# A fused decoder layer: the first turns of the attention pipeline in another order

## The chip, the core and the metric

The kernel runs on one core of a Trainium2 chip. A core has five engines, each with an instruction stream of its own: TensorE (PE in the rows; its weight loads are PEld), VectorE (DVE), ScalarE (ACT), GpSimd (POOL) and SyncE (SP), which here only issues DMAs. DMAs issued by SP, ACT and POOL are shown with a "q" behind the engine's name. The metric is the device time of one launch in microseconds, less is better. One execution was also recorded by the profiler; all views below read that one.

## The reference, cut to what matters

```
x = x + attn(layernorm(x))                 # x: 64 sequences, 128 tokens, width 128
x = x + xattn(layernorm(x), ctx_1024)      # context: 64 x 77 tokens, width 128, mask
x = x + ffn(layernorm(x))                  # 8 experts, the best 2 for each token
# attn and xattn: 16 heads of width 8
scores = einsum('bqhd,bkhd->bhqk', q, k)
attn   = softmax(scores)
out    = einsum('bhqk,bkhd->bqhd', attn, v) @ Wff.T + bff
```

## The kernel before

The 64 sequences are cut into 16 blocks of 4. Every block goes through a software pipeline of "turns": `steps` calls `body(t, t % 2)` on every engine for t = -3 to 17. A turn has two halves, x and y. In the x half of turn t TensorE does self-attention's shifted scores, and the products with the values, of block t beside the unshifted scores of block t + 1, of which VectorE takes the row maxima. In the y half it does the same for cross-attention: block t - 2 beside the maxima of block t - 1. `in_x(u)` and `in_y(u)` put the small work of other stages behind unit u (of 16) of a half: layer norm, transposes, projections, the gate. I write m(b), s(b), cm(b) and c(b) for the maxima and the attention proper of block b, in self-attention (m, s) and cross-attention (cm, c).

The way of one block into m(b), in self-attention:

1. SP loads `xin`; DVE `stats`, POOL `power`, ACT `normalise`; PE turns it over (`x1T`) and multiplies by w_q and w_k.
2. ACT, DVE, ACT and POOL (`first`, `remainder`, `second`, `third`) write each of q and k as three bf16 parts. SP `dump`s them to DRAM (`stk_q`, `stk_k`) and reads them back with `stack`, six DMAs each, in another layout into `qkbig` (`qs`, `ks`): rows 0 to 47 hold the parts of half of the heads, rows 64 to 111 those of the other half.
3. Three more rows of `ks` hold ones (`ones_under`). PE computes the scores of m(b) in 16 units of 4 matmuls of 128 columns (`scores`, two PSUM banks by turns), DVE reduces each unit (`maxima`).
4. POOL splits the negated maxima into three bf16 parts (`shares`), PE turns them over (`maxima_T`), ACT copies them to `parts_m`, and six DMAs (`fold`, or `first_folds` on ACT's queue for blocks 0 and 1) write them under `qs`. Only then can s(b) start: its scores (`shifted`) come out of PE with the maximum already taken off. ACT takes the exponentials (`attend`), PE multiplies by the values (`values`).

Cross-attention does the same with `cks` and `cqs` (`stack_cross`). The places of `cks` that hold an identity are written once by POOL (`places`). `gate` computes three small products that the router needs from the weights alone; before, it runs at the end of turn -1. Each engine runs its stream in order, so a wait holds back all that is behind it.

## Time and profile before

| | us |
|---|---|
| median of 3 runs | 1080.31 |
| the three runs | 1078.13, 1080.31, 1083.88 |
| time of the profiled execution | 1077.14 |
| its span (first to last instruction) | 1075.4 |
| PE busy in it | 904.4 (84%) |
| ACT busy | 796.5 (74%) |
| DVE busy | 781.5 (73%) |

The span is what the rows below cover; the profiled execution's own time is 1.7 us longer than its span and 3.2 us under the median. Busy PE time counts pipelined matmuls whose ends are modelled, so 84% doesn't say that PE is at its peak.

### The profile page before, as it was taken

How to read it: one execution, taken by the hardware profiler on the slowest of the kernel's cores; microseconds unless marked ns; L12 is line 12 of the kernel's file. 1: busy time of each engine (PE TensorE's matmuls, PEld its weight loads, DVE VectorE, ACT ScalarE, POOL GpSimd, SP SyncE). 2: the span in 40 equal slices, each digit the busy share in tenths (PEclk: the TensorE clock that was granted, in tenths of full speed). 3: DMA queues.
4: the chain of work that ended last, by engine and by line, in shares of the span. 5: the costliest groups of instructions: out<-in, count | busy, mean ns of one | idle time of the engine just before them, and what ended most of it. 6: DMA issues, size and time to landing. Idle time of an engine off the chain costs nothing.

```text
span 1075.4 us, 30453 instructions
## 1 busy us (share of the span) xinstructions
PE 904.4 (84%) x11109; PEld 661.0 (61%) x11109; DVE 781.5 (73%) x2190; ACT 796.5 (74%) x1652; POOL 648.1 (60%) x837
## 2 busy tenths in 40 slices
PE   2675778898998999889899888887878899999992
PEld 1343546666666666566576566665666677887771
DVE  3553756777886887877877768657638998998883
ACT  2153567778787878778788776777678899999981
POOL 2353333456676676766766654646556677777885
PEclk9996989999999999999999998999989999999996
DMA  4628877756777777677677664447223467779884
GB/s 99 133 56 158 149 122 151 164 111 146 167 128 150 156 137 158 136 139 162 127 152 152 128 129 100 91 128 153 65 63 102 150 212 237 248 209 255 233 225 127
DMA packets 108140, 158.82 MB, mean 148 GB/s; under 512 B 16829, under 2 KB 82000, under 8 KB 103384
## 3 DMA queue, kind: packets, MB, share of 16 engines
q1 hardware_dynamic: 93624, 130.25, 53.7%
q0 software_dynamic: 11184, 24.02, 9.2%
q10 hardware_dynamic: 3184, 2.60, 0.8%
q8 instruction: 89, 1.46, 0.6%
q14 instruction: 59, 0.48, 0.2%
HBM read 103.12 MB, written 53.78 MB: 146 GB/s over the span
## 4 chain that ended last, share of the span: by engine, by line
PE 50%; DVE 17%; DMA 9%; ACT 8%; issue 8%; POOL 5%; ACTq 1%; SPq 1%; POOLq 0%; DVEq 0%
PE pv L1799 8%; PE sc_m L1774 6%; PE wb L1751 6%; PE wb L1757 5%; PE wb L1746 4%; PE sc_a L1785 4%; DMA xg<-xs_d 3%; DVE negm_m L1185 3%; DVE on L1199 2%; DVE negm_cm L1185 2%; PE pv L2035 2%; PE pv L2028 2%; PE pv L2029 2%; DMA cbig<-parts_m 2%; ACT probs L934 2%
## 5 line engine op out<-in xcount | busy, mean ns | idle before, releaser
L934 ACT ACTIVATE probs<-sc_a 77x512 f32<-77x512 f32 (+1 forms) x512 | 302.1, 597 | 95.0 <-PE sc_a L1785 90.0
L689 POOL DMA_INDIRECT y_d<-yo,row x156 | 170.0, 1090 | 64.0 <-issue 41.6
L1185 DVE TENSOR_REDUCE negm_m<-sc_m 128x4 f32<-128x512 f32 x256 | 170.7, 683 | 42.7 <-PE sc_m L1774 39.9
L680 POOL DMA_INDIRECT xs_d<-xrow,slot_i x128 | 135.7, 1060 | 107.9 <-PE sc_a L1785 68.7
L1185 DVE TENSOR_REDUCE negm_cm<-sc_m 128x4 f32<-128x308 f32 x256 | 116.4, 471 | 77.9 <-PE sc_m L1774 76.2
L1799 PE MATMUL pv<-probs,big 128*32 128x128 f32 x4096 | 169.2, 284 | 3.9 <-issue 3.8
L1400 DVE TENSOR_TENSOR gl<-g,gh 128x512 fp32r<-128x512 f32 x156 | 107.0, 687 | 34.2 <-ACT g L1083 33.8
L1774 PE MATMUL sc_m<-qkbig 48*128 48x128 bf16 x1024 | 104.8, 233 | 26.9 <-DVE negm_m L1185 15.4
L1799 PEld LDWEIGHTS pv<-probs,big 128*32 128x32 f32 x4096 | 98.9, 111 | 38.8 <-ACT probs L934 12.6
L1774 PEld LDWEIGHTS sc_m<-qkbig 48*128 48x128 bf16 x1024 | 61.6, 100 | 94.9 <-DVE negm_m L1185 49.6
L1785 PE MATMUL sc_a<-qkbig 51*128 51x128 bf16 x1024 | 103.0, 227 | 8.6 <-ACT probs L934 7.2
L1785 PE MATMUL sc_a<-cbig 128*77 128x128 bf16 x1024 | 100.5, 222 | 1.9 <-ACT probs L934 1.5
L1774 PE MATMUL sc_m<-cbig 125*128 125x77 bf16 x1024 | 79.2, 200 | 14.7 <-DVE negm_cm L1185 8.1
L1774 PEld LDWEIGHTS sc_m<-cbig 125*128 125x128 bf16 x1024 | 59.6, 98 | 31.7 <-DVE negm_cm L1185 19.1
L1785 PEld LDWEIGHTS sc_a<-cbig 128*77 128x77 bf16 x1024 | 69.1, 118 | 4.7 <-ACT probs L934 3.4
L2035 PE MATMUL pv<-gl,vh 128*128 128x512 f32 x156 | 65.7, 421 | 5.9 <-DVE gl L1400 5.9
L1785 PEld LDWEIGHTS sc_a<-qkbig 51*128 51x128 bf16 x1024 | 60.1, 98 | 14.2 <-ACT probs L934 11.9
L668 POOL TENSOR_TENSOR parts_q<-rest_q,parts_q 128x512 bf16<-128x512 f32 x16 | 24.5, 1534 | 68.1 <-ACT parts_q L916 68.1
L1083 ACT ACTIVATE gh<-sc_m,bias 128x512 fp32r<-128x512 f32 x78 | 54.1, 693 | 13.8 <-issue 6.6
L2028 PE MATMUL pv<-gh,vh 128*128 128x512 f32 x156 | 62.0, 397 | 1.2 <-ACT gh L1083 1.0
L636 POOL TENSOR_SCALAR lnve<-lnmv 128x4 f32<-128x4 f32 x48 | 13.6, 284 | 79.9 <-DVE lnmv L1164 78.0
L2029 PE MATMUL pv<-gh,vl 128*128 128x512 f32 x156 | 61.3, 393 | 0.0
(240 smaller groups left out, 2302.6 us busy)
## 6 DMA issues: line engine op xcount, KB each, us to landing
wraw<-W_dram SPq DMA_DIRECT2D x39, 516.0 KB, 5.0
xg<-xs_d SPq DMA_DIRECT2D x39, 260.0 KB, 3.3
stk_q<-parts_q SPq DMA_DIRECT2D x16, 384.0 KB, 2.5
stk_k<-parts_k SPq DMA_DIRECT2D x16, 384.0 KB, 2.7
qkbig<-stk_q SPq DMA_DIRECT2D x32, 192.0 KB
qkbig<-stk_k SPq DMA_DIRECT2D x32, 192.0 KB
stk_cq<-parts_cq SPq DMA_DIRECT2D x16, 384.0 KB, 2.7
cbig<-stk_cq SPq DMA_DIRECT2D x32, 192.0 KB
```

The source lines that it names most:

```text
L680: nc.gpsimd.indirect_dma_start(out=xs_d, in_=xrow[b % 2][:, c // 2, c % 2, :], in_offset=None, out_offset=bass.IndirectOffsetOnAxis(ap=slo ...
L689: nc.gpsimd.indirect_dma_start(out=y12_d, in_=yo[i % NY][:, c, :], in_offset=None, bounds_check=2 * B * S - 1, oob_is_err=False, out_offse ...
L934: nc.scalar.activation(probs[e % 4][0:rows], sc_a[e % 2][0:rows], ACT.Exp, scale=scale)\
L1185: nc.vector.tensor_reduce(out=negm[n][:, s, HG * g + 4 * half:HG * g + 4 * half + 4], in_=sc_m[u % 2][:, 0:4 * cols].rearrange("p (j k) -> ...
L1400: nc.vector.tensor_tensor(out=gl[c], in0=g[c], in1=hi32(gh[c]), op=ALU.subtract).then_inc(gl_ok.sem, 1)
L1751: nc.tensor.matmul(wb[BANK[n]][:, 0:cols], lhsT, rhs, start=True, stop=True).then_inc(filled[n].sem, 1)
L1774: i = nc.tensor.matmul(sc_m[u % 2][:, j * cols:(j + 1) * cols], qst[rows, slot + j, s * S:(s + 1) * S], kst[rows, slot + j, s * cols:(s + ...
L1785: i = nc.tensor.matmul(sc_a[u % 2][0:cols, j * S:(j + 1) * S], kst[rows, slot + j, s * cols:(s + 1) * cols], qst[rows, slot + j, s * S:(s ...
L1799: i = nc.tensor.matmul(pv[s // 2][VW * c:VW * (c + 1), slot * S:(slot + 1) * S], va[:, HG * s + 4 * half + c, g, :], probs[u % 4][:, c * S ...
L2028: nc.tensor.matmul(o, vh[par][:, w], gh[c], start=(c == 0), stop=False)
L2029: nc.tensor.matmul(o, vl[par][:, w], gh[c], start=False, stop=False)
L2035: nc.tensor.matmul(y_banks[par][:], vh[par][:, c * 128:(c + 1) * 128], gl[c], start=False, stop=(c == FC - 1)).then_inc(w2_done.sem, 1)
```

## The change

Only the first turns are reordered:

- m(0) stays in the x half of turn -1, and m(1) follows in its y half, alone. m(0)'s `maxima_T` and fold come behind the third unit of m(1), and v of block 1 behind its thirteenth.
- Turn 0: x half s(0), alone on PE's side of the scores, with `maxima_T` of block 1 behind its second unit of shifted scores; y half s(1), beside the small work of block 0. Block 1's fold goes through SP's queue instead of ACT's.
- Turn 1: x half m(2), alone; then `maxima_T` of block 2, now ahead of cm(0); y half cm(0).
- From turn 2 on the order is the old one.
- `gate` moves from the end of turn -1 to the end of turn 0, the bias product with it.
- The ones rows of `ks` and `cks` are written first, in `constants`, and `xin` of block 1 is loaded between them instead of behind `dump("k", 0)`. The two copies of `places` move from turn -1 to turns -3 and -2.
- In turn 0 block 2's turning over, q and k come earlier (`FIRST_SELF`), and ck(0) behind k(2) on POOL; ck(0) is stacked earlier in SP's order. ACT waits for the last dump of q or k before it writes `parts_q` or `parts_k` again, in every turn.

```diff
--- before.py
+++ after.py
+SELF = dict(turn=8, q=10, k=13)
+FIRST_SELF = dict(turn=4, q=6, k=9)
+NORM1_OF = {0: 0}
...
+        def self_of(t):
+
+            return FIRST_SELF if t == 0 else SELF
+
+        def turned_maxima(t):
+
+            return {-1: 3, 1: 0}[t] if t in (-1, 1) else 7
...
+                    sp.wait_ge(ident_ok.sem, 7)
+                    for b in range(2):
+                        for g in range(NG):
+                            ones_under(ks[b], GP * g + KS, slice(0, HG))
+                        if b == 0:
+                            sp.wait_ge(ln_ok["1"].sem, ln_ok["1"].val(0))
+                            sp.dma_start(xin[:], x_v[1]).then_inc(x_in.sem, 16)
+                    for b in range(2):
+                        for g in range(NG):
+                            ones_under(cks[b], CS, slice(g * HG, (g + 1) * HG))
...
+                            if (n, t) != ("ck", 1):
+                                stack_cross(n, t - 1, dst[1 - par])
+                    if t == 0:
+                        fold(1, qs[1])
...
+                    if on_(t + 3) and t + 3 != 1:
...
+                    if t == 0:
+                        stack_cross("ck", 0, cks[0])
...
-                    if on_(t + 1):
+                    if t == 0:
+                        third("ck", t)
+                        mask_rows(t)
+                    if on_(t + 1) and t != 0:
...
+                    if t == -1:
+                        shares("m", 1)
...
-                steps(pool, body, {-2: numbers, -1: first_spare})
+                steps(pool, body, {-3: first_places, -2: numbers, -1: first_spare})
...
+                        if t == 0 and u == 3:
+                            evac(parts["m"][:], "m", 1, 0, rows=3 * H)
...
+                        if u == self_of(t)["q"] and on_(t + 2):
+                            if t + 2 >= 1:
+                                act.wait_ge(dumped["q"].sem, dumped["q"].val(t + 1))
...
-                    attend("s", t, 128, float(D) ** -0.5, in_x)
+                    attend("s", t if t != 1 else NONE, 128, float(D) ** -0.5, in_x)
...
-                    attend("c", t - 2, SC, float(DH) ** -0.5, in_y)
+                    if t == 0:
+                        attend("s", 1, 128, float(D) ** -0.5, in_y)
+                    else:
+                        attend("c", t - 2, SC, float(DH) ** -0.5, in_y)
...
-                    maxima("m", t + 1, S, in_x_too if t != -1 else None)
+                    maxima("m", t + 1 if t != 0 else NONE, S, in_x_too if t != -1 else None)
...
-                    maxima("cm", t - 1, SC, in_y)
+                    if t == -1:
+                        dve.wait_ge(split["m"].sem, split["m"].val(0, 2))
+                        maxima("m", 1, S, in_y)
+                    else:
+                        maxima("cm", t - 1, SC, in_y)
...
+                        if t == 0 and u == 2:
+                            maxima_T("m", 1)
...
-                    if on_(t):
-                        pe.wait_ge(drained["v"].sem, drained["v"].val(t))
-                        pe.wait_ge(stacked["m"].sem, stacked["m"].val(t))
-                        attn = ("s", t, qs[par], ks[par], vaug[par], S, ("c", t - 3))
-                    if on_(t + 1):
-                        for n in ("q", "k"):
-                            pe.wait_ge(stacked[n].sem, stacked[n].val(t + 1))
-                        if isinstance(t, int) and t + 1 < 2:
-                            pe.wait_ge(ones_in.sem, ones_in.val(t + 1))
-                        maxi = ("m", t + 1, qs[1 - par], ks[1 - par], S)
+                    if on_(t) and t != 1:
+                        attn = self_attention(t, ("c", t - 3) if t != 2 else ("s", 1))
+                    if on_(t + 1) and t != 0:
+                        maxi = self_maxima(t + 1)
...
+                    if t == -1:
+                        maxi = self_maxima(1)
+                    if t == 0:
+                        attn = self_attention(1, ("s", 0))
+                    if t == 1:
+                        maxima_T("m", 2)
...
-                steps(pe, body, {-1: gate})
+                steps(pe, body, {0: gate})
```

What stands in PE's stream behind m(0), before. `negm_m`'s splitting (`m_split`) is POOL's, `sc_m` are the scores for maxima, `sc_a` the shifted ones; L1824 is `maxima_T`, L1757 v of block 1, L1953 to L1958 the gate:

```order
L1774 MATMUL sc_m<-qkbig 128x128 [waits m_max_ok]
L1774 MATMUL sc_m<-qkbig 128x128 x3
L1824 MATMUL wb<-identb,third_m 48x128 [waits m_split,k_drained,m_max_ok]
L1824 MATMUL wb<-identb,third_m 48x128 x3
L1757 MATMUL wb<-w_v,xnT 128x128 [waits m_drained]
L1757 MATMUL wb<-w_v,xnT 128x128 x3
L1953 MATMUL wb<-ident,sim_u 128x8 [waits gate_set,v_drained]
L1955 MATMUL wb<-simT,wp_n 128x8 [waits gate_ev]
L1958 MATMUL wb<-cw_o,scrap 128x128 [waits gate_set,gate_ev]
L1774 MATMUL sc_m<-qkbig 128x128 [waits q_stacked,k_stacked,m_stacked,ones_in,v_drained,gate_set]
L1774 MATMUL sc_m<-qkbig 128x128 x7
L1785 MATMUL sc_a<-qkbig 128x128 x4
```

The same place of the changed kernel (L1822 are scores for maxima, L1886 is `maxima_T`):

```order
L1822 MATMUL sc_m<-qkbig 128x128 [waits m_max_ok]
L1822 MATMUL sc_m<-qkbig 128x128 x3
L1822 MATMUL sc_m<-qkbig 128x128 [waits k_stacked,ones_in,q_stacked,m_max_ok]
L1822 MATMUL sc_m<-qkbig 128x128 x7
L1822 MATMUL sc_m<-qkbig 128x128 [waits m_max_ok]
L1822 MATMUL sc_m<-qkbig 128x128 x3
L1886 MATMUL wb<-identb,third_m 48x128 [waits m_split,k_drained]
```

PE goes from m(0) to m(1) with a wait for block 1's q and k alone, and the maxima of block 0 are turned over three units later.

Between s(1) and m(2), the end of turn 0 in the changed kernel; L1847 are the products with the values, L2017 to L2022 the gate:

```order
L1799 MATMUL wb<-xnT,cw_q 128x512 [waits x2T_drained]
L1847 MATMUL pv<-probs,big 32x128 [waits exp_s_ok]
L1847 MATMUL pv<-probs,big 32x128 x3
L1847 MATMUL pv<-probs,big 32x128 [waits exp_s_ok]
L1847 MATMUL pv<-probs,big 32x128 x3
L2017 MATMUL wb<-ident,sim_u 128x8 [waits gate_set,v_drained]
L2019 MATMUL wb<-simT,wp_n 128x8 [waits gate_ev]
L2022 MATMUL wb<-cw_o,scrap 128x128 [waits gate_set,gate_ev]
L1822 MATMUL sc_m<-qkbig 128x128 [waits k_stacked,q_stacked,gate_set]
L1822 MATMUL sc_m<-qkbig 128x128 x7
```

The gate's three products now stand between the last product of turn 0 and the first scores of m(2), which wait for `gate_set`.

SP's stream from the last constant on, before:

```order
L423 DMA temp_b<-temp_dram 128x1
L428 DMA stk_q<-parts_q 128x3x512 [waits q_part3]
L428 DMA stk_k<-parts_k 128x3x512 [waits k_part3]
L491 DMA xin<-x_dram 128x4x128 [waits ln1_ok]
L447 DMA qkbig<-stk_q 24x4096 [waits q_dumped]
```

and in the changed kernel:

```order
L435 DMA temp_b<-temp_dram 128x1
L455 DMA qkbig<-ones 3x32x128 [waits ident_ok]
L455 DMA qkbig<-ones 3x32x128
L442 DMA xin<-x_dram 128x4x128 [waits ln1_ok]
L455 DMA qkbig<-ones 3x32x128 x2
L455 DMA cbig<-ones 3x32x77 x4
L450 DMA stk_q<-parts_q 128x3x512 [waits q_part3]
L450 DMA stk_k<-parts_k 128x3x512 [waits k_part3]
L466 DMA qkbig<-stk_q 24x4096 [waits q_dumped]
```

The load of `xin` for block 1 has moved ahead of both dumps, with eight small DMAs around it.

## Rows read from the trace of the kernel before

**Rows 1.** Busy time by stage; columns: stretch, length, busy us (instructions), clock, DMA, GB/s.

```profile
62.00:80.00 18.00, 17.11 (x274) 10.70 (x274) 12.04 (x19) 14.03 (x29) 5.16 (x6) 1.00 0.12 38
80.00:99.30 19.30, 7.25 (x36) 4.24 (x35) 5.39 (x22) 5.51 (x11) 7.77 (x15) 0.75 0.81 152
99.30:119.60 20.30, 18.19 (x278) 11.56 (x279) 14.15 (x23) 14.68 (x30) 6.23 (x6) 0.82 0.78 135
119.60:138.50 18.90, 11.49 (x104) 8.02 (x105) 11.89 (x38) 5.36 (x11) 7.16 (x15) 0.79 0.80 161
160.80:181.00 20.20, 18.28 (x304) 14.17 (x306) 11.88 (x38) 13.94 (x27) 6.11 (x12) 1.00 0.74 148
```

**Rows 2.** The chain that ended last, early part: start us, us, what.

```profile
88.91 10.32 DMA qkbig<-parts_m
...
125.94 10.95 DMA qkbig<-stk_k
...
138.48 0.60 PE sc_m L1774 x8
```

**Rows 3.** SP's DMA issues: start us, us, what.

```profile
20.36 0.38 SPq L428 DMA_DIRECT2D stk_k<-parts_k  x1
...
21.31 2.38 SPq L447 DMA_DIRECT2D qkbig<-stk_q  x6
...
27.39 1.29 SPq L447 DMA_DIRECT2D qkbig<-stk_k  x3
...
119.99 0.38 SPq L428 DMA_DIRECT2D stk_k<-parts_k  x1
...
121.67 2.37 SPq L447 DMA_DIRECT2D qkbig<-stk_q  x6
...
141.07 1.68 SPq L433 DMA_DIRECT2D cbig<-ones  x2
```

**Rows 4.** One stretch of 1 us, columns as in Rows 1.

```profile
37.00:38.00 1.00, 0.72 (x9) 0.38 (x8) 0.00 (x0) 0.60 (x1) 0.09 (x1) 1.00 0.00 0
```

**Rows 5.** PE in order of time: start us, us, what, [idle before, releaser].

```profile
37.60 0.62 PE L1774 MATMUL sc_m<-qkbig 48*128 48x128 bf16 x8 [0.28 <-issue]
...
51.18 0.59 PE L1824 MATMUL wb<-identb,third_m 128*48 128x128 bf16 x4 [2.25 <-POOL third_m L659]
52.45 2.08 PE L1757 MATMUL wb<-w_v,xnT 128*128 128x128 f32 x8 [0.68 <-ACT parts_m L888]
57.20 0.27 PE L1953 MATMUL wb<-ident,sim_u 8*128 8x8 f32 x1 [2.67 <-ACT big L1002]
...
61.96 0.30 PE L1774 MATMUL sc_m<-qkbig 48*128 48x128 bf16 x2 [2.56 <-issue]
```

**Rows 6.** PE at the start of turn 2's y half.

```profile
160.83 0.30 PE L1774 MATMUL sc_m<-cbig 125*128 125x77 bf16 x4 [1.26 <-DMA cbig<-parts_m]
```

**Rows 7.** DVE around the end of m(0) and the gate.

```profile
38.66 11.00 DVE L1185 TENSOR_REDUCE negm_m<-sc_m 128x4 f32<-128x512 f32 x16
49.58 0.86 DVE L1159 BATCH_NORM_STATS2 lnst<-xin 128x6 f32<-128x128 f32 x4
...
59.44 0.29 DVE L1672 TENSOR_TENSOR bo_b<-bo_b,wb 128x128 f32<-128x128 f32 x1 [3.89 <-PE wb L1958]
```

**Rows 8.** POOL's preset of the cks tiles.

```profile
53.01 8.53 POOL L794 COPY cbig<-identb 77x4928 bf16<-77x4928 bf16 x2
```

**Rows 9.** ACT's two roundings behind cross-attention's q product.

```profile
95.26 0.69 ACT L897 ACTIVATE parts_cq<-wb,bq_c 128x512 bf16<-128x512 f32 x1 [2.23 <-PE wb L1751]
96.83 0.63 ACT L916 ACTIVATE parts_cq<-rest_q 128x512 bf16<-128x512 f32 x1 [0.89 <-DVE rest_q L1175]
```

**Rows 10.** PE, matmuls of m(2) and s(1) side by side.

```profile
100.69 0.29 PE L1774 MATMUL sc_m<-qkbig 48*128 48x128 bf16 x1 [0.36 <-DVE negm_m L1185]
100.70 0.29 PE L1785 MATMUL sc_a<-qkbig 51*128 51x128 bf16 x1
```

**Rows 11.** The end of turn 1's y half, columns as in Rows 1.

```profile
130.50:136.00 5.50, 4.39 (x20) 2.16 (x18) 2.15 (x6) 2.55 (x7) 3.64 (x5) 0.50 0.80 141
```

More of the change, by code:

```diff
@@ L451, in stack_cross @@
                     sp.wait_ge(dumped[n].sem, dumped[n].val(b))
-                    if n == "ck" and b < 2:
-                        for g in range(NG):
-                            ones_under(n, dst, CS, slice(g * HG, (g + 1) * HG))
                     for place, skip in RUNS:
@@ L754, in body @@
                         third("q", t + 2)
-                    if on_(t):
+                    if on_(t) and t > 0:
                         third("ck", t)
@@ L947, in in_x @@
                     def in_x(u):
-                        if 2 <= u < 2 + NS and on_(t + 2):
-                            normalise("1", t + 2, xin, u - 2)
+                        if t == 0 and u == 3:
+                            evac(parts["m"][:], "m", 1, 0, rows=3 * H)
+                        at = NORM1_OF[t] if t in NORM1_OF else 2
+                        if at <= u < at + NS and on_(t + 2):
+                            normalise("1", t + 2, xin, u - at)
                         if u == 4 and on_(t - 3):
@@ L964, in in_x @@
                             fold(t - 2, cqs[par])
-                        if u == 8 and on_(t + 2):
+                        if u == self_of(t)["turn"] and on_(t + 2):
                             evac(xnT["1"][:], "x1T", t + 2, 0)
@@ L1109, in gate @@
                     nc.scalar.activation(wpx[:, D:D + E], wb[0][:, 0:E], ACT.Copy).then_inc(gate_ev.sem, 1)
-                steps(act, body, {-1: gate})
+                steps(act, body, {0: gate})
                 def last_block(i, c):
@@ L1292, in in_x @@
                             divide("c", t - 3, u)
-                        if u in MASKS and on_(t - 1):
+                        if u in MASKS and on_(t - 1) and t != 1:
                             masks(t - 1, cqs[1 - par], MASKS.index(u))
@@ L1299, in in_x @@
                             stats("3", t - 3, x3)
-                        if u == 11 and on_(t + 2):
+                        if u == self_of(t)["q"] + 1 and on_(t + 2):
                             wait_block(dve, part3["cq"], t - 1)
@@ L1305, in in_x @@
                             remainder("ck", t, bk_c)
-                        if u == 14 and on_(t + 2):
+                        if u == self_of(t)["k"] + 1 and on_(t + 2):
                             wait_block(dve, part3["k"], t + 1)
@@ L1310, in in_y @@
                     def in_y(u):
+                        if t == 0 and u in MASKS:
+                            masks(0, cqs[0], MASKS.index(u))
                         if u < NO and on_(t):
@@ L1672, in output_bias, with beside_context @@
                     nc.vector.tensor_tensor(out=bo_b[:], in0=bo_b[:], in1=wb[0][:, 0:D], op=ALU.add).then_inc(gate_set.sem, 1)
-                def beside_and_bias():
+                def beside_context():
                     ones_beside(cvaug, "cv", SC)
-                    output_bias()
-                steps(dve, body, {-3: beside_first, -2: gate, -1: beside_and_bias})
+                steps(dve, body, {-3: beside_first, -2: gate, -1: beside_context, 0: output_bias})
                 def late_base():
@@ L1818, in beside, with self_attention, self_maxima @@
                             between(u)
+                def self_attention(b, last):
+                    pe.wait_ge(drained["v"].sem, drained["v"].val(b))
+                    pe.wait_ge(stacked["m"].sem, stacked["m"].val(b))
+                    return "s", b, qs[b % 2], ks[b % 2], vaug[b % 2], S, last
+                def self_maxima(b):
+                    for n in ("q", "k"):
+                        pe.wait_ge(stacked[n].sem, stacked[n].val(b))
+                    if b < 2:
+                        pe.wait_ge(ones_in.sem, ones_in.val(3))
+                    return "m", b, qs[b % 2], ks[b % 2], S
                 def maxima_T(n, b):
@@ L1860, in in_x @@
                             maxima_T("cm", t - 2)
-                        if u == 8 and on_(t + 2):
+                        if t == 0 and u == 2:
+                            maxima_T("m", 1)
+                        if u == self_of(t)["turn"] and on_(t + 2):
                             pe.wait_ge(ln_ok["1"].sem, ln_ok["1"].val(t + 2))
@@ L1886, in in_y @@
                             project("s", t, w_ff)
-                        if u == 6 and on_(t + 1):
+                        if u == turned_maxima(t) - 1 and on_(t + 1) and t not in (0, 1):
                             maxima_T("m", t + 1)
```

58 lines of the change are left out of this document (29 added, 29 removed).

## The prediction

> **What bounds the kernel now.** I read the profile's page first, then windows by stage, the chain of waits, SP's DMA issues and PE's stream in order of time. The page gives PE 84% of the span, but that is an average over 20 turns, and the change touches only those that end by about 181 us. So the question is: when does turn 2 begin, before and after? Behind it the order of work is the old one, and what shifts its start shifts the end.
>
> [Rows 1] show stages of two kinds. In those in which two halves' work lies side by side (62 to 80, 99.3 to 119.6, 160.8 to 181) PE is busy for 17.11 to 18.28 of 18 to 20.3 us: PE-bound. In 80 to 99.3 PE works 7.25 of 19.30 us and DMA is at 0.81: that is the wait for block 1's fold, which the chain of waits shows as 10.32 us of DMA [rows 2]. In 119.6 to 138.5 DMA is at 0.80 again, and the chain goes through 10.95 us of block 3's q and k being stacked before turn 2's x half starts at 138.48 [rows 2]. So before turn 2 the kernel is bound by turns by PE and by the transfers that PE's next half needs.
>
> The first stage is a DMA stage too. SP begins to stack block 0's q at 21.31 [rows 3], the DMA engines go quiet at 37 [rows 4], and m(0) begins at 37.60 [rows 5]: 16.3 us from the first stack issue to PE. For block 3 the same took from 121.67 [rows 3] to at most 138.48, at which PE starts [rows 2]: at most 16.8, and by the end of the chain's DMA (125.94 + 10.95 = 136.89) 15.2. I use 15.2 to 16.3 as the price of stacking a block.
>
> **The change, step by step.** Times are those of PE from the start of the span.
>
> 1. *xin(1) and the ones rows first.* Before, xin(1) is issued between k(0)'s dump (20.36) and the first stack (21.31) [rows 3], and shares the 16 engines with the stacks of block 0. Now it goes some 11 us earlier, when they have little to do. Its 128 x 4 x 128 x 4 bytes are 0.26 MB; the twelve stacks move 96 rows of 4096 x 2 bytes for each of q and k, 1.57 MB. So xin is 14% of the 1.84 MB, 2.3 of 16.3 us; with one issue less ahead of the stacks I take 2.5: m(0) starts at 35.1. Bounds: 0 (the packets of the stacks themselves set the time) and 3. The ones DMAs are small; two cost SP 1.68 us of issue [rows 3], 0.84 each. All eight now lie ahead of the dumps, where SP otherwise waits.
>
> 2. *m(1) behind m(0).* m(0) took 37.60 to 49.66 (38.66 + 11.00, [rows 5, 7]), 12.1 us. With 12.1 it now ends at 47.2. Block 1's q and k come out about 6 us earlier than before, because their input does, and their first stack issue falls at about 36; plus 15.2 to 16.3 gives 51.2 to 52.3; I take 51.7 for m(1)'s start. So PE waits some 4.5 us there. m(1) costs the 12.1 less 0.7 for its first unit, whose results DVE need not wait for, plus v of block 1 (2.08 us of PE in [rows 5], of which I take 1.4; bounds 0.7 and 2.1) and block 2's layer norm statistics on DVE (0.86, [rows 7], up to 1.3 with what waits for it): about 14.0, so it ends at 65.7 to 66. Fold(0) needs m(0)'s maxima_T behind the third unit of m(1): it lands near 61, hidden behind m(1).
>
> 3. *x half of turn 0: s(0) alone.* It took 18.0 with m(1) beside it [rows 1]. What m(1) gave up is less than its count of instructions: in [rows 10] a score matmul of m and one of s start 0.01 us apart on different partitions and take 0.29 each, so they ran side by side and splitting them gives little back. New in this half is maxima_T of block 1, which waits for POOL's shares; after m(0) it waited 2.25 us from the last product and began 1.5 behind the last maximum (49.66 to 51.18, [rows 5, 7]), so I add 1.3 when two units of s(0) are ahead of it, less what the missing evictions give. I take 18.3; bounds 16.5 and 19.5. End: 84.3. Fold(1) is issued near 70 and takes at most the 10.32 of [rows 2]: landed by 84. This is the change's gain: the 19.30 us of 80 to 99.3 held 12 us without PE work.
>
> The Trainium skill, TensorEngine Tiling (Array Packing), Overview, says that the array can work as several independent tiles, up to twice as fast for contractions of 64 rows or fewer. By that rule taking m and s apart costs up to all of m's matmuls again, 64 of 0.29 us, where a reader who adds up busy time would expect the total to stay. The trace agrees for these two.
>
> 4. *y half of turn 0: s(1) beside in_y(0).* The nearest full half is 160.8 to 181, 20.20 us [rows 1], in which the scores of cm ran too: 16 units of 0.30 [rows 6] are 4.8. That gives 15.4; I take 15.7, bounds 15 and 17. End: 100.0.
>
> 5. *gate.* Before, it stood in a gap that was there anyway: its first product at 57.20 came 2.67 us after v for want of ACT, DVE's end of it is at 59.44 + 0.29 = 59.73, and s(0) waited for the fold until 61.96 [rows 5, 7]. Cover gone, its price is 59.73 − 57.20 = 2.5, and ahead of it on ACT stands now the rounding of cq (the two of [rows 9] are 1.57 us from start to start, PE idle 2.23 before the first), of which 1.3 shows. Together 3.8; bounds 2.5 and 4.7. Queued behind it on PE is m(2), which waits for gate_set. Block 2's stack has landed by 100 to 102, so the gate and not the DMA sets m(2): 103.8, that is 4.5 later than before (99.3).
>
> 6. *x half of turn 1: m(2) alone*, beside in_x: 12.1 of m(0) is its floor, and in_x adds transposes and the projections of block 3. I take 15; bounds 13.3 and 17. End 118.8. k(3)'s dump lay 0.4 us behind the end of this half (119.99 against 119.6, [rows 1, 3]). ACT's and DVE's chain to it doesn't shrink as much as PE's, so I take 1.7 behind: 120.5.
>
> 7. *maxima_T(2) ahead of cm(0).* It waits for POOL's third of k and then the shares: +3.3 (the 1.5 of m(0), and 1.8 of POOL work ahead of it; bounds 1.5 and 4.5), to 122.1. Then cm(0), which before took from 119.6 to about 136 [rows 1, 11]: 16.3, so PE would be ready at 138.4. The DMA way is later by a little: from dump to x(2) 138.48 − 119.99 = 18.5 [rows 2, 3], so 120.5 + 18.5 = 139.0. Fold(2), issued near 124 and 10 long, is hidden.
>
> 8. *The rest.* The two ones DMAs at 141.07 (1.68, [rows 3]) leave turn 2; its y half began after 1.26 us of waiting for cbig's DMA [rows 6], so −1.0, bounds 0 and −1.26. ACT's new wait for the dumps in every turn: it is there for a transfer that was issued a turn's part earlier, +0.3 in all, bounds 0 and 1.7. `places` (8.53, [rows 8], 4.27 each) goes to turns in which POOL only waits for input: nothing; if the cover were gone, 4.3 on block 1's third parts, which would eat most of the 4.5 us that m(1) already waits.
>
> Sum: +0.5 (139.0 against 138.5) − 1.0 + 0.3 = −0.2. The profiled execution's 1077.14 becomes 1076.9. It lies 3.2 under the median of the three runs, so the forecast for a median is 1080.31 − 0.2 = **1080.1 us**. In words: 12 us of PE's waiting at 80 to 99.3 are bought with a wait of 4.5 ahead of m(1), two gaps at the gate and maxima_T (7.1), and a turn whose start goes by DMA as before.
>
> **The rivals.** What a measurement of this kernel can tell from no change is about 0.5%, 5.4 us: faster is below 1074.9, slower above 1085.7.
>
> *Faster: block 1 lands early, and the lone halves are short.* If a landing goes by the last stack issue rather than by bytes, m(1) starts 2.2 us earlier (49.5); s(0) alone takes 16.5 instead of 18.3, and m(2) 13.3 instead of 15. That is −5.7, and it reaches turn 2 because k(3)'s dump comes with m(2)'s end: 1080.1 − 5.7 = 1074.4, and 1071.5 with the gate at its low end as well. For it: the lone halves lack half of PE's instructions (274 in 18 us, [rows 1]). Against: ACT's exponentials alone are 14 us of each s half [rows 1], and [rows 10]. It begins to count as faster when all three terms hold. Chance 0.22.
>
> *Slower: TensorE at half clock in m(2) and cm(0).* Granted clock is 0.75 and 0.79 in the stages in which PE waits, and 0.50 at 130.5 to 136 [rows 1, 11]: the lower of its two levels, 1.2 of 2.4 GHz, after PE had worked 7.25 of 19.30 us or 11.49 of 18.90. The change gives turn 1 two PE-light halves in a row with the gate's gap ahead of them. Then m(2) takes 17, not 15, the gate's gap 4.7, maxima_T 4.5, and x(2) starts on a low clock, +1 to +2: +5 to +6.5, some 1085.1 to 1086.6. It decides from about 5.6 us on. Chance 0.14.
>
> The Trainium skill, TensorE: Matmul & The Clock Gate, says that TensorE's clock is gated to 1.2 GHz when it is idle. By that rule this rival is what the gate gap and the two lone halves invite; the granted clock in the rows falls after idle stretches, which agrees.
>
> *It doesn't do what it says: turn 2 is fixed by block 3's stack.* If k(3)'s dump depends on xin(3) and the projections rather than on PE's order, x(2) starts within 1 us of 138.5 whatever came before: 1079 to 1081. Chance 0.10.
>
> **How the numbers follow.** The forecast as summed has 0.52, its own range 1077 to 1084 (step 1 at 0: +2.5; steps 3, 4 and 6 at either end partly cancel). With the last rival and 0.02 for the rest, within 0.5% has 0.64, faster 0.22, slower 0.14. The range from 1071.5 to 1086.5 leaves about 0.1 out at each end.
>
> **What the changed profile would show.** m(0) near 35.1 and m(1) near 51.7, with a wait for DMA between; s(0) at 66, s(1) at 84.3 with no DMA wait; a gap of 2.5 to 4.7 us with the gate in it, its releasers ACT and DVE, and m(2) at 103.8; maxima_T(2) waiting for POOL at 119 to 122; x(2) at 139.0 released by DMA, or PE. The prediction is wrong if m(1) starts before 49 or after 55, if a lone half takes as long as a double one (20 us), if m(2) is released by a stack, or if x(2) starts more than 5 us from 138.5. It is wrong in another way if x(2) starts there and the end moves all the same: then a wait was added in every turn.

## The result: about 1% slower

| | us |
|---|---|
| changed kernel, median of 4 runs | 1094.28 (1090.35, 1091.42, 1097.13, 1097.86) |
| kernel before, median of 4 runs beside it | 1082.10 (1078.13, 1080.31, 1083.88, 1089.56) |
| ratio | 1.0098, 95% interval 1.0051 to 1.0145 |
| profiled execution of the changed kernel | 1090.35, span 1088.6 |

The interval lies wholly above 1: 5.5 to 15.7 us more. Ratios here and below leave out runs more than 1.5% above their kernel's fastest. The kernel before had medians of 1084 us beside the first eight of the further runs, 1105 beside the next three and 1109 beside the last, so times are only compared with those taken beside them. The profiled executions are 13.2 us apart, and turn 2 starts 10.1 us later (138.48 to 148.56), so most of the difference is there when the order becomes the old one again. The rest, 3 us, is less than the runs of one kernel differ by.

I read the changed kernel as the prediction laid it out, PE in order of time. First its wait for block 1 (compare [rows 5]):

```profile
37.77 0.62 PE L1822 MATMUL sc_m<-qkbig 48*128 48x128 bf16 x8 [6.31 <-issue]
...
54.76 0.62 PE L1822 MATMUL sc_m<-qkbig 48*128 48x128 bf16 x8 [6.08 <-DMA qkbig<-stk_k]
...
67.38 0.39 PE L1822 MATMUL sc_m<-qkbig 48*128 48x128 bf16 x2 [0.77 <-DVE negm_m L1228]
67.49 0.37 PE L1833 MATMUL sc_a<-qkbig 51*128 51x128 bf16 x2
```

m(0) starts when it did before (37.60 then, 37.77 now), PE waits 6.08 us for block 1's k, and s(0) begins at 67.49 against 61.96. SP shows why m(1) can't be earlier:

```profile
20.64 2.33 SPq L466 DMA_DIRECT2D qkbig<-stk_q  x6
23.02 2.22 SPq L466 DMA_DIRECT2D qkbig<-stk_k  x6
31.26 0.39 SPq L450 DMA_DIRECT2D stk_q<-parts_q  x1
34.88 0.38 SPq L450 DMA_DIRECT2D stk_k<-parts_k  x1
35.31 0.48 SPq L510 DMA_DIRECT2D xin<-x_dram  x1
38.38 2.14 SPq L466 DMA_DIRECT2D qkbig<-stk_q  x6
```

Block 0's stack takes 20.64 to 37.77 and block 1's 38.38 to 54.76: one behind the other, 17.1 and 16.4 us. SP issues the second only when m(0)'s first unit is done (its wait on `max_f` stands in the code of both kernels).

The end of turn 0, with the gate in the open, and the end of turn 1:

```profile
103.01 1.10 PE L1799 MATMUL wb<-xnT,cw_q 128*128 128x512 f32 x2 [0.31 <-ACT xnT L921]
104.03 0.64 PE L1847 MATMUL pv<-probs,big 128*32 128x128 f32 x16
104.61 0.22 PE L2017 MATMUL wb<-ident,sim_u 8*128 8x8 f32 x1
106.46 0.39 PE L2019 MATMUL wb<-simT,wp_n 128*128 128x8 f32 x2 [1.63 <-ACT simT L1150]
107.11 0.79 PE L2022 MATMUL wb<-cw_o,scrap 128*128 128x128 f32 x2 [0.27 <-ACT wpx L1152]
108.29 0.61 PE L1822 MATMUL sc_m<-qkbig 48*128 48x128 bf16 x8 [0.38 <-DVE bo_b L1721]
...
125.28 0.62 PE L1822 MATMUL sc_m<-qkbig 48*128 48x128 bf16 x8
130.52 0.59 PE L1886 MATMUL wb<-identb,third_m 128*48 128x128 bf16 x4 [4.62 <-POOL third_m L679]
...
146.03 1.10 PE L1799 MATMUL wb<-xnT,cw_q 128*128 128x512 f32 x2 [0.64 <-ACT xnT L921]
148.56 0.41 PE L1822 MATMUL sc_m<-qkbig 48*128 48x128 bf16 x8 [1.43 <-issue]
```

From the last product of turn 0 to m(2) there are 3.7 us; from the last unit of m(2) to the turned-over maxima PE waits 4.62 us for POOL. By stage, cut at the starts of the halves (columns as in [rows 1], to which they answer):

```profile
54.76:67.38 12.62, 9.98 (x73) 6.57 (x73) 10.21 (x23) 1.68 (x3) 1.71 (x4) 1.00 0.03 8
67.38:86.90 19.52, 16.40 (x218) 9.79 (x219) 6.90 (x9) 14.32 (x29) 8.64 (x11) 1.00 0.24 78
86.90:104.60 17.70, 14.81 (x223) 9.92 (x222) 7.01 (x25) 12.75 (x26) 4.45 (x9) 1.00 0.76 155
104.60:108.30 3.70, 1.42 (x10) 0.94 (x7) 1.03 (x2) 2.85 (x9) 1.88 (x2) 0.84 0.05 12
108.30:126.00 17.70, 15.86 (x86) 8.49 (x86) 10.33 (x17) 4.10 (x9) 2.86 (x3) 0.50 0.56 106
126.00:130.50 4.50, 0.00 (x0) 0.01 (x1) 1.81 (x3) 0.39 (x2) 3.56 (x7) 0.50 0.35 122
```

Two rows carry the result. s(0) alone takes 19.52 us; with m(1) beside it the half took 18.00 [rows 1]. And m(2) alone, 86 matmuls where the shared half of before had 278, takes 17.70 us at a granted clock of 0.50. The halves that were thinned did not become short. For s(0)'s half ScalarE (14.32 us busy of 19.52) doesn't explain all: PE also waited 1.82 us for POOL at 70.23, ahead of block 1's turned-over maxima, and a group of 16 products with the values took 1.08 us at 71.31 and 74.50, and 0.64 from 77.35 on; before, the groups took 0.64 already from 69.19 on. No run takes these apart.

### The profile page after: what moved, and what is told of

The parts are those of the page before. It is cut to its first block, busy times and chain, and to the rows that moved or that the text cites. A ratio compares the mean times of both kernels' runs of the same rounds, so it can differ in the third digit from the quotient of the medians.

```text
span 1088.6 us, 30485 instructions
## 1 busy us (share of the span) xinstructions
PE 923.4 (85%) x11109; PEld 674.9 (62%) x11109; DVE 786.0 (72%) x2190; ACT 795.7 (73%) x1652; POOL 646.5 (59%) x837
## 4 chain that ended last, share of the span: by engine, by line
PE 52%; DVE 17%; issue 9%; ACT 8%; POOL 6%; DMA 5%; SPq 2%; ACTq 1%; POOLq 0%; DVEq 0%
PE pv L1847 8%; PE sc_m L1822 7%; PE wb L1799 6%; PE wb L1805 5%; PE sc_a L1833 4%; PE wb L1794 4%; DVE negm_m L1228 2%; DVE negm_cm L1228 2%; DVE on L1242 2%; DMA xg<-xs_d 2%; PE pv L2099 2%; PE pv L2093 2%; PE pv L2092 2%; ACT probs L967 2%; DVE lnst L1202 1%
## 5 line engine op out<-in xcount | busy, mean ns | idle before, releaser
L1847 PE MATMUL pv<-probs,big 128*32 128x128 f32 x4096 | 169.1, 285 | 2.2 <-issue 2.2
L1822 PE MATMUL sc_m<-qkbig 48*128 48x128 bf16 x1024 | 106.2, 239 | 35.3 <-DVE negm_m L1228 17.3
L1822 PEld LDWEIGHTS sc_m<-qkbig 48*128 48x128 bf16 x1024 | 62.1, 102 | 101.7 <-DVE negm_m L1228 51.8
L1847 PEld LDWEIGHTS pv<-probs,big 128*32 128x32 f32 x4096 | 99.1, 111 | 38.8 <-ACT probs L967 12.9
L1833 PE MATMUL sc_a<-qkbig 51*128 51x128 bf16 x1024 | 99.7, 227 | 8.6 <-ACT probs L967 8.3
L1822 PE MATMUL sc_m<-cbig 125*128 125x77 bf16 x1024 | 80.2, 203 | 10.6 <-DVE negm_cm L1228 7.8
L1822 PEld LDWEIGHTS sc_m<-cbig 125*128 125x128 bf16 x1024 | 60.9, 100 | 27.5 <-DVE negm_cm L1228 19.2
L1833 PEld LDWEIGHTS sc_a<-qkbig 51*128 51x128 bf16 x1024 | 58.2, 97 | 20.2 <-ACT probs L967 16.3
L659 POOL TENSOR_TENSOR lnrs<-lnve,mhalf 128x4 f32<-128x4 f32 x48 | 55.2, 1150 | 4.0
```

The source lines that it names most:

```text
L1822: i = nc.tensor.matmul(sc_m[u % 2][:, j * cols:(j + 1) * cols], qst[rows, slot + j, s * S:(s + 1) * S], kst[rows, slot + j, s * cols:(s + ...
L1833: i = nc.tensor.matmul(sc_a[u % 2][0:cols, j * S:(j + 1) * S], kst[rows, slot + j, s * cols:(s + 1) * cols], qst[rows, slot + j, s * S:(s ...
L1847: i = nc.tensor.matmul(pv[s // 2][VW * c:VW * (c + 1), slot * S:(slot + 1) * S], va[:, HG * s + 4 * half + c, g, :], probs[u % 4][:, c * S ...
```

## The experiments

Theory at the start: the loss is a sum of exposed work in turns -1 to 1 (m(1) alone, the gate, the clock), carried to the end. Rivals: the gate or the early maxima alone do it; ACT's new waits cost in every turn; turn 2 is pinned by transfers whatever precedes it. Nothing separates kernels here better than 0.3 to 0.5%, so I read each twice: the ratio to the kernel before, and the places in its profile. One profile is one execution; where the clock fell in it moves the later places by some us (last section).

**The gate between m(0) and m(1).** In each engine's stream the call moves to turn -1:

```diff
                     if t == -1:
+                        gate()
                         maxi = self_maxima(1)
...
-                steps(pe, body, {0: gate})
+                steps(pe, body)
```

> The changed kernel with the gate (and the bias product and its addition) between m(0) and m(1), where PE waits 6.1 us for block 1's k; all else as changed. Theory (the gate's 3.7 us between s(1) and m(2) lie on the path, and the clock's fall at 107 us comes with that pause): m(2) starts at 104.6 to 105 in place of 108.29, turn 2's x half 3.7 to 8 us before the changed kernel's 148.56, the time 4 to 8 us under the changed kernel's 1090 to 1098. Rival (turn 2 is fixed by the transfers of block 3, whatever stands ahead): m(2) earlier, but x(2) within 1 us of 148.56 and no change of time. Second rival (the gate's wait is not hidden in the new place either): m(1) later than 54.76 by 1 us or more.

Ratio to the kernel before 1.0139 (1.0061 to 1.0218).

```profile
48.78 0.27 PE L2021 MATMUL wb<-ident,sim_u 8*128 8x8 f32 x1 [0.79 <-DVE negm_m L1230]
49.32 0.60 PE L2023 MATMUL wb<-simT,wp_n 128*128 128x8 f32 x2 [0.27 <-ACT simT L1152]
50.18 0.79 PE L2026 MATMUL wb<-cw_o,scrap 128*128 128x128 f32 x2 [0.27 <-ACT wpx L1154]
55.14 0.62 PE L1825 MATMUL sc_m<-qkbig 48*128 48x128 bf16 x8 [4.17 <-DMA qkbig<-stk_k]
...
104.56 2.04 PE L1802 MATMUL wb<-xnT,cw_q 128*128 128x512 f32 x2 [0.24 <-ACT xnT L921]
106.53 1.08 PE L1850 MATMUL pv<-probs,big 128*32 128x128 f32 x16
107.55 0.62 PE L1825 MATMUL sc_m<-qkbig 48*128 48x128 bf16 x8
```

The gate disappears in the wait for DMA, and m(2) follows the values without a pause. But it starts at 107.55, only 0.7 earlier: in this execution the clock fell at the end of turn 0 already, and cq's product takes 2.04 in place of 1.10. So the clock does not need the gate's pause to fall, and that half of the theory is gone. The next two runs have the gate where the change put it, and there too it read 0.50 from about 103 us on, before the gate. The gate's price is seen against the next run, where the clock fell as early: m(2) at 111.45 there, 107.55 here, 3.9 us. In the time it can't be seen.

**Block 2's maxima turned over in cm(0) again.**

```diff
-            return {-1: 3, 1: 0}[t] if t in (-1, 1) else 7
+            return 3 if t == -1 else 7
...
-                    if t == 1:
-                        maxima_T("m", 2)
```

> The changed kernel with the turned-over maxima of block 2 back behind the seventh unit of cm(0) in place of ahead of cm(0). Theory (turn 2's start is fixed by the stacks of block 3 and the fold of block 2, which land at 147.2 and 148.6 and which SP issues only from 130.7 on): cm(0) starts 4.5 us earlier, at 126.0 to 126.5 in place of 131.05, but x(2) stays within 1.5 us of 148.56, and the time within 0.3% of the changed kernel's. Rival (the 4.62 us that PE waits for POOL's third_m are on the path): x(2) at 144 to 145 and the time 4 to 5 us less.

Ratio 1.0100 (1.0062 to 1.0137), the changed kernel's own. The scores of cm(0) come 1.40 us after those of m(2), not 4.6, and PE then waits at the end for what it gained:

```profile
128.14 0.39 PE L1822 MATMUL sc_m<-qkbig 48*128 48x128 bf16 x4 [0.44 <-DVE negm_m L1228]
129.94 0.44 PE L1822 MATMUL sc_m<-cbig 125*128 125x77 bf16 x4 [1.40 <-DVE negm_m L1228]
...
144.39 1.10 PE L1799 MATMUL wb<-xnT,cw_q 128*128 128x512 f32 x2 [0.63 <-ACT xnT L921]
150.67 0.62 PE L1822 MATMUL sc_m<-qkbig 48*128 48x128 bf16 x8 [5.18 <-issue]
```

5.18 us of waiting stand ahead of turn 2 where the changed kernel has 1.43. But m(2) itself began 3.2 us later in this execution (111.45), so turn 2 at 150.67 is outside the 1.5 us that the theory gave it. Counted from m(2) it comes 39.2 us behind, 40.3 in the changed kernel and 39.0 in the run with the gate moved, which has the pause too: the pause of 4.62 us cost nothing that can be seen.

**Unused matmuls in the pauses.** 26 behind the gate's first product and 40 ahead of `maxima_T`:

```diff
+                def keep_busy(n):
+                    for _ in range(n):
+                        nc.tensor.matmul(sc_a[0][:, 0:128], identb[:], identb[:], start=True, stop=True)
```

> The changed kernel with matmuls that compute nothing that is used: 26 of 128x128 in bf16 behind the gate's first product and 40 ahead of the turned-over maxima of block 2, both into a PSUM bank that is free then, so that PE does not pause there. Theory (m(2) takes 17.7 us because the granted clock is 0.50 in it, and the clock fell because PE paused at the gate): the clock record stays 1.00 in m(2), whose length falls to 13 to 14.5 us; x(2) 3 to 5 us earlier than 148.56. Rival (the clock falls for another reason, or m(2) is bound by DVE and ACT and not by PE's clock): m(2) still 17 to 18 us long, or the clock at 1.00 and the length unchanged; the time the same or up to 2 us more.

Ratio 1.0150 (1.0090 to 1.0210), an interval that overlaps the changed kernel's. m(2)'s half, cut at 112.2 and 130:

```profile
112.20:130.00 17.80, 15.19 (x80) 8.04 (x78) 11.16 (x18) 4.45 (x9) 2.39 (x3) 0.53 0.59 102
```

The clock is 0.53, and m(2) itself, 111.84 to 129.12, takes 17.3 us. In this execution the clock fell at about 103, ahead of the gate; behind the 26 unused matmuls it read 1.00 again from 110 to 112, and from 114 on 0.50: filling the pauses didn't keep the clock up. The rival holds as far as the pauses go. What the half would take at the full clock stays untried, but in the four profiles in which this half holds the same work, it is the shorter the higher its mean clock: 17.6 us at 0.50 (the changed kernel), 17.3 at 0.54 (here), 17.1 at 0.57 (maxima late), 16.3 at 0.60 (gate moved). That speaks for the clock having a part in its length; it isn't tested by itself.

**Ones rows and xin first, alone**, in the kernel before (with ACT's waits for the dumps):

```diff
+                    sp.wait_ge(ident_ok.sem, 7)
+                    for b in range(2):
+                        for g in range(NG):
+                            ones_under(ks[b], GP * g + KS, slice(0, HG))
+                        if b == 0:
+                            sp.wait_ge(ln_ok["1"].sem, ln_ok["1"].val(0))
+                            sp.dma_start(xin[:], x_v[1]).then_inc(x_in.sem, 16)
...
+                                act.wait_ge(dumped["q"].sem, dumped["q"].val(t + 1))
```

> The kernel before with one part of the change alone: the ones rows written first, xin of block 1 loaded between them, and ACT's wait for the dumps of q and k (in every turn), which that order needs. The order of the turns, the gate and the places are those of before. Theory (these parts cost nothing, the order of the first turns does): the time within 0.4% of before, x(2) at 137 to 139.5 against 138.48, m(0) at 37.2 to 38 against 37.60. Rival (ACT's new wait is paid in every turn and explains the distance that grows behind turn 2): the time 3 us or more above before, with ACT's idle time before the first part of q or k released by a dump, in each turn.

> The kernel before with the ones rows and xin of block 1 first, a second time, with more rounds: is it faster than before, or the same? Theory (turn 2 starts 2 us sooner): the time 1 to 3 us under before. Rival: no difference that can be measured.

Ratios 0.9965 (0.9915 to 1.0016) and 1.0014 (0.9980 to 1.0048): no difference that can be measured. So neither the early ones, nor xin, nor ACT's waits in every turn explain the loss. m(0) stays at its place, but s(0) comes 2.8 us earlier than before, and turn 2 at 136.09 and 136.76 against 138.48 (the first theory had it at 137 or later):

```profile
58.02 0.79 PE L1966 MATMUL wb<-cw_o,scrap 128*128 128x128 f32 x2 [0.27 <-ACT wpx L1117]
59.20 0.62 PE L1782 MATMUL sc_m<-qkbig 48*128 48x128 bf16 x8 [0.38 <-DVE bo_b L1680]
...
96.73 0.62 PE L1782 MATMUL sc_m<-qkbig 48*128 48x128 bf16 x8 [2.86 <-DMA qkbig<-parts_m]
```

**The wait that the change removes, removed alone.** In the kernel before, ACT writes block 1's rows at the start of turn 0, from block 0's maxima:

```diff
+                    if t == 0:
+                        act.wait_ge(stacked["m"].sem, stacked["m"].val(0))
+                        first_folds(0, qs[1])
                     attend("s", t, 128, float(D) ** -0.5, in_x)
```

> The kernel before without the wait that the change removes: the rows that block 1's shifted scores need are written early, at the start of turn 0, from block 0's maxima (so block 1's attention is computed with the wrong maximum; its output is not the reference's). Theory (behind the fold another wait of the same length stands: block 2's stack, which lands at 98.6 us against the fold's 99.2, and ahead of both in_y(0)'s own chain, whose last product on PE ends at 95.2): turn 1's x half starts at 98 to 99.3, at most 1.5 us earlier than 99.32. Rival (the step of the prediction that counted 12 us of the 19.30 as a gain): it starts at 92 or earlier.

One run: 1076.56, beside a median of 1083.76 (1075.15 to 1108.20) for the kernel before. (A softmax doesn't depend on which number is taken off a row, so what is computed differs only in rounding.) The end of the stage, before:

```profile
93.18 2.05 PE L1751 MATMUL wb<-xnT,cw_q 128*128 128x512 f32 x2 [0.78 <-ACT xnT L888]
99.32 0.62 PE L1774 MATMUL sc_m<-qkbig 48*128 48x128 bf16 x8 [4.10 <-DMA qkbig<-parts_m]
```

and in this run:

```profile
94.00 2.04 PE L1756 MATMUL wb<-xnT,cw_q 128*128 128x512 f32 x2 [0.78 <-ACT xnT L888]
100.14 0.62 PE L1779 MATMUL sc_m<-qkbig 48*128 48x128 bf16 x8 [4.09 <-DMA qkbig<-stk_k]
```

This is the row of the study. The fold's wait is gone, and PE waits 4.09 us for block 2's k instead; turn 1 starts at 100.14, not earlier than the 99.32 of before. The edit has a cost of its own: ScalarE now issues the six DMAs at 61.19 (3.91 us), inside s(0)'s half, and that half's last copy (`oT`) comes at 81.30 instead of 79.69. From that copy to turn 1 it is 18.84 us against 19.63, so in its own stage the wait was worth 0.8 us, and not 12.

**And block 2's q and k earlier too** (as `FIRST_SELF` does in the change):

```diff
+            return {0: dict(turn=4, q=6, k=9)}.get(t, dict(turn=8, q=10, k=13))
```

> As the run without block 1's fold (its output is not the reference's for the same reason), and turn 0's turning over, q and k of block 2 four units earlier, as in the change, with ck(0) behind k(2) on POOL. Theory (with the fold and the stack both out of the way, in_y(0)'s chain from DVE's divisions to PE's cq product is what is left of the 19.3 us): turn 1's x half starts at 95 to 97, right behind the cq product, 2 to 4 us before 99.32 and no more. Rival (turn 1 waits for the transfers only): 91 to 94, before the cq product is due.

```profile
93.51 2.05 PE L1763 MATMUL wb<-xnT,cw_q 128*128 128x512 f32 x2 [0.78 <-ACT xnT L894]
95.81 0.62 PE L1786 MATMUL sc_m<-qkbig 48*128 48x128 bf16 x8 [0.26 <-DMA qkbig<-stk_k]
```

With both waits out of the way turn 1 starts 0.3 us behind the last product of `in_y(0)`, at 95.81: in_y(0)'s own chain of small work fills what is left. Turn 1 is 3.5 us earlier than before, and from the copy of `oT` (80.80) to turn 1 it is 15.0 us, 4.6 less: that is what both waits together were worth. And it wasn't kept: turn 2 came at 140.19, later than before, and the one run took 1081.01.

**Block 3's q and k earlier in turn 1**, in the changed kernel and in the kernel before with xin first:

```diff
-            return FIRST_SELF if t == 0 else SELF
+            return FIRST_SELF if t == 0 else dict(turn=5, q=7, k=10) if t == 1 else SELF
```

> The changed kernel with block 3's turning over, q and k three units earlier in turn 1 (5, 7, 10 in place of 8, 10, 13) and ck(1) behind k(3) on POOL. Theory (from the start of m(2) to turn 2 it takes 38.7 to 41 us in every kernel so far, with s(1) in that half or not, because k(3) comes out of in_x at unit 13 and its dump, stack and the fold behind it then take 19): k(3)'s dump comes 2.5 to 4 us sooner after m(2)'s start, and turn 2's x half 36 to 37.5 us behind m(2)'s start; the time 2 to 4 us under the changed kernel's. Rival (turn 1 is bound by PE at half clock and the pauses): 39 to 41 us from m(2) to turn 2 as before.

> The kernel before with the ones rows and xin of block 1 first (as in the run that had these alone) and, in turn 1 alone, q and k of block 3 three units earlier (5, 7, 10 in place of 8, 10, 13) with ck(1) behind k(3) on POOL; the order of the halves is that of before. Theory (turn 2's start hangs on block 3's stack): turn 2's x half 36 to 37.5 us behind turn 1's instead of 39, at 133 to 135.5 us, and the time 3 to 6 us under the kernel before. Rival (in_y(1)'s chain or cm(0) bounds turn 1's y half): 38.5 to 39.5 us behind and a time within 0.3% of before.

Ratios to the kernel before 1.0091 (1.0055 to 1.0126) and 0.9972 (0.9934 to 1.0010): no change against their bases. Neither theory held; the rivals came closer (turn 2 is 40.3 and 39.8 us behind turn 1). In the first, k(3)'s dump is issued 17.8 us behind m(2)'s start in place of 20.9, but turn 2 starts at 147.95, 40 us behind m(2), since PE runs through its own work without a wait before it. In the second the shared half took longer:

```profile
96.00:118.50 22.50, 19.95 (x258) 11.95 (x259) 14.02 (x23) 14.20 (x29) 6.53 (x6) 0.67 0.63 126
```

So my theory that turn 1's 39 us hang on k(3) fell: with k(3) earlier, PE at a low clock (0.67 in this row) had no idle time ahead of turn 2 to give back.

**m(1) ahead of s(0), but s(1) back beside m(2)** (gate ahead of m(1), maxima as before):

```diff
-                    if on_(t) and t != 1:
-                        attn = self_attention(t, ("c", t - 3) if t != 2 else ("s", 1))
+                    if on_(t):
+                        attn = self_attention(t, ("c", t - 3))
...
-                    if t == 0:
-                        attn = self_attention(1, ("s", 0))
```

> One half of the reordering alone: m(1) stays ahead of s(0), alone behind m(0), as in the change; but s(1) goes back beside m(2) in turn 1's x half, as before, so that the y half of turn 0 holds only in_y(0). The gate stands ahead of m(1) and block 2's maxima are turned over behind the seventh unit of cm(0), so that neither weighs here. Theory (taking m(1) out of s(0)'s half costs about 5 us at s(0) and is not given back, since s(0) alone is no shorter than with m(1); moving s(1) costs the rest): s(0) at 67 to 68.5, turn 1's x half at 102 to 105, when block 2's stack has landed, against 99.7 before and 108.3 to 112 in the kernels with the whole reordering; turn 2's x half 39 to 41 us behind that, at 142 to 145; the time 3 to 6 us above before. Rival (the loss is all in m(1)'s new place): turn 2's x half at 147 or later, the time 10 us above before.

Ratio 1.0075 (1.0040 to 1.0110).

```profile
66.44 0.62 PE L1822 MATMUL sc_m<-qkbig 48*128 48x128 bf16 x8
67.83 0.39 PE L1822 MATMUL sc_m<-qkbig 48*128 48x128 bf16 x2 [0.77 <-DVE negm_m L1227]
...
101.36 2.05 PE L1799 MATMUL wb<-xnT,cw_q 128*128 128x512 f32 x2 [0.78 <-ACT xnT L921]
103.34 0.62 PE L1822 MATMUL sc_m<-qkbig 48*128 48x128 bf16 x8
...
142.34 0.62 PE L1822 MATMUL sc_m<-qkbig 48*128 48x128 bf16 x8 [2.21 <-issue]
```

The profile's places are the theory's: s(0) at 67.8, turn 1 at 103.3, turn 2 at 142.3. By the time, this half of the reordering costs 0.75%, 4.4 to 12.2 us at the 1105 that the kernel before took beside it: both the theory's upper end and the rival's 10 are inside. What is safe is that m(1)'s new place makes the kernel slower without s(1)'s; its 0.75% is three quarters of the changed kernel's 0.98%, though the intervals overlap, and the two were timed beside different runs of the kernel before.

**ck(0) stacked at the end of turn 0**, on top of xin first, twice:

```diff
+                    if t == 0:
+                        stack_cross("ck", 0, cks[0])
```

> The kernel before with the ones rows and xin of block 1 first, and block 0's ck stacked in SP's stream at the end of turn 0, as in the change, in place of the start of turn 1 (DMA engines have less to do then, and cm(0) waits for cq's stack, which goes behind it). Theory (turn 2 hangs on block 3's stack, not on cm(0)): cm(0) up to 2.5 us earlier than in the kernel with xin first alone, turn 2's x half within 1 us of it, the time within 0.3% of it. Rival (turn 1 is one row of transfers, each behind the other): turn 2's x half 2 us or more earlier, the time 2 us less.

> The kernel before with the ones rows and xin of block 1 first and block 0's ck stacked at the end of turn 0, a second time: the first time it was 0.7% faster than before, though turn 2 began no earlier. If the gain is real the ratio is again 0.990 to 0.997; if the first one was chance, its interval holds 1. The theory (turn 2's start decides) has no place for a gain here: it expects turn 2's x half at 136 to 139 and no difference.

Ratios 0.9930 (0.9893 to 0.9968) and 0.9962 (0.9928 to 0.9995): both intervals below 1. This is the one version that came out faster than both kernels, by some 0.4 to 0.7%. Its size isn't known better than that: the plain medians are 1101.34 and 1105.08 in the first round (0.9966), 1103.53 and 1109.49 in the second (0.9946). The cause is not shown: turn 2 began at 138.1 in the first profile and at 145 in the second, neither earlier than before, so the theory that turn 2's start decides has no place for it.

## Why the prediction was wrong

It gave 1080.1 us and 64% for no change; the ratio is 1.0098. The chain of steps to turn 2 said 139.0; it was 148.56. Of that, by its own steps:

| step | before | forecast | measured | late by |
|---|---|---|---|---|
| 1, 2: m(1) starts | | 51.7 | 54.76 | 3.1 |
| 2: m(1) to s(0) | | 14.3 | 12.6 | -1.7 |
| so s(0) starts | 62.0 | 66.0 | 67.4 | 1.4 |
| 3: s(0) alone | 18.0 | 18.3 | 19.5 | 1.2 |
| 4: s(1) beside in_y(0) | 19.3 | 15.7 | 17.7 | 2.0 |
| 5: gate in the open | | 3.8 | 3.7 | -0.1 |
| 6: m(2) alone | 20.3 | 15.0 | 17.6 | 2.6 |
| 7: end of m(2) to turn 2 | 18.9 | 20.2 | 22.7 | 2.5 |

"Before" is the half that stood in the same place. Steps 4 and 6 are the gain of the change: s(1) goes into the half with the wait, and the next half loses it. The forecast had 8.9 us for the two (3.6 and 5.3), they gave 4.3 (1.6 and 2.7). The costs (s(0) starting later, steps 3, 5 and 7) were forecast at 9.4 and came to 14.4. So of the 9.6 us by which the sum was off, 4.6 are the gain and 5.0 the costs.

- **The step that failed is the gain, stated in step 3** ("the 19.30 us of 80 to 99.3 held 12 us without PE work") **and booked in steps 4 and 6**: 8.9 us forecast, 4.3 measured. An engine that is idle for 12 us in a stage isn't waiting 12 us for the transfer that ends last. In the kernel before, cq's product ends at 95.23 and only then PE waits for the fold, 4.10 us; the other 8 are pauses inside in_y(0)'s chain (DVE, ACT, POOL and PE by turns; the longest, 4.51, for ACT's `xn`). And behind the fold stood block 2's stack, 4.09 us when the fold is gone. So the change removed a wait worth 0.8 us by itself, and 4.6 with the stack moved too. s(1) did fill the pauses (PE busy 14.81 of 17.70 us, before 7.25 of 19.30), but the half became only 1.6 us shorter, and m(2)'s only 2.7. Against this it paid for m(1) alone. Which engine's chain sets the 17.7 us isn't shown. The prediction had the pieces (PE busy 7.25 of 19.30) and read them as a reserve.
- **Step 1, m(0) 2.5 us earlier**: not so (37.77 against 37.60). Its lower bound of 0 was right: with xin's 0.26 MB gone from the front, block 0's stack still took 17.1 us from first issue, so xin's bytes don't set it. The early xin did bring block 1's parts forward, as forecast, but its stack waits for block 0's: SP holds it until m(0)'s first unit. The price of 15.2 to 16.3 us for a stack was right (16.4 for block 1).
- **Steps 4 and 6** were too short by 2.0 and 2.6 us, both beyond the stated bounds (17 each). For step 6 the rival "TensorE at half clock in m(2)" had the mechanism: 0.50 through the whole half. It gave this 0.14; in the five profiles of kernels with m(2) alone its units take 16.3 to 18.9 us, so it was the likely case. Its price was 2 us in m(2), and m(2) took 2.6 more than forecast; how much of that is the clock isn't shown. The rival put the fall down to the gate's pause, and neither moving the gate nor filling the pause kept the clock up. The Trainium skill, TensorE: Matmul & The Clock Gate, Part 1: The HAM clock gate, has an idle TensorE fall to 1.2 GHz. The rows agree in so far as the clock is low in the stages with little PE work (0.75 and 0.79 in [rows 1]), while in the run with the gate moved it fell in a half in which PE was busy for 16.89 of 19.71 us.
- **Step 5** was right, 3.7 against 3.8, and by two profiles 3.9.
- **Step 7**: maxima_T(2) waited 4.6, not 3.3, but with it moved back PE only waits longer for turn 2, so that pause isn't what made the step 2.5 us late. What did stays open; PE's clock was 0.50 at the step's start.
- **Step 8** was right in kind: turn 2's x half went from 22.4 us (138.48 to 160.83 [rows 2, 6]) to 20.8 (148.56 to 169.38), 1.5 us for the ones rows and the wait behind them; ACT's waits in every turn showed no cost.
- The rival "it doesn't do what it says: turn 2 is fixed by block 3's stack" was wrong. Turn 2 follows turn 1 by 39 to 41 us in 12 of the 14 profiles (42.5 and 44.4 in the others), but turn 1 itself moved.
- The range's upper end, 1086.5, came from a case in which the steps' other bounds held. All four large terms were late at once.
- The sum of the rival "faster" has a slip: 1074.4 with the gate at its low end (2.5 in place of 3.8) is 1073.1, not 1071.5.
- Of its own signs of being wrong one came true: turn 2 starts more than 5 us from 138.5. m(1) at 54.76 and s(0)'s 19.5 us stayed just inside their bounds, and m(2) was released by DVE's end of the gate, not by a stack.

The size: s(0) began 5.5 us later than before and 8.3 later than with xin first alone (67.49 against 59.20); m(1) alone takes a half of 12.6 us, of which 7.1 lie ahead of 61.96, where PE had only the gate and its waits before, and s(0) without it gives nothing back. The second half of the reordering, s(1) beside in_y(0), then adds a few us in the profiles (m(2) at 107.6 with the gate out of the way, 103.3 without s(1) in that half); by the times the two can't be told apart. The 3 us that the profiles differ behind turn 2 stay open as well.

## What to carry to other kernels

Before a wait is removed, ask what the engine would wait for next: the last releaser in the chain is the only one shown, and here block 2's stack landed within 1 us of it, and in_y(0)'s own chain ended only 4 us ahead. Measure the wait from the last instruction that the engine still has to do, not as the stage's idle time. Before work is lifted out of a half that it shares, ask what else sets that half's length: here m(1) left s(0)'s half and it took 19.5 us in place of 18.0; s(1) left m(2)'s and it took 17.6 in place of 20.3. What is lifted out needs a half of its own, and only what waited there before comes off its price.

## What the runs showed of the hardware

- TensorE's granted clock fell in the first turns of every profile, at another place each time. Its mean from 80 to 150 us was 0.78 before, 0.78 in the changed kernel, 0.73 with the gate moved and 0.71 with xin first alone, so it doesn't sort the kernels by their times. With one and the same kernel (ck(0) stacked early) the shared half of turn 1 had 0.83 and turn 2 began at 138.1 in one profile; the other had this in turn 0's y half and the shared half:

```profile
80.00:103.00 23.00, 10.57 (x60) 7.05 (x57) 5.40 (x22) 5.82 (x11) 8.51 (x15) 0.59 0.88 157
103.00:125.00 22.00, 21.06 (x272) 12.83 (x269) 14.31 (x23) 14.61 (x29) 5.49 (x6) 0.65 0.44 90
```

  Turn 2 began 7 us later there. A difference of a few us at one place of one profile is therefore no proof here; the text above leans on such places only where several profiles agree.
- The same product (`wb<-xnT,cw_q`, 128x512 in f32, two matmuls) took 1.10 us at 103.01 in the changed kernel, where the clock reads 1.00, and 2.04 at 104.56 with the gate moved, where it reads 0.50.
- The clock that the windows show isn't the whole speed: from 54.76 to 67.38 us it reads 1.00, yet the v product in it (`wb<-w_v,xnT`, 8 matmuls) took 2.07 us there, at 63.98, and 1.16 at 96.62, where it reads 1.00 as well. So a group of matmuls that comes again and again is a better witness than the record.
- Two blocks' stacks, issued one behind the other, took 17.1 and 16.4 us, and a stack whose xin was out of the way took as long as one with it (17.1 us from 20.64 to 37.77, before 16.3 from 21.31 to 37.60).
